# Gate and up projections by Strassen's seven block products, with rows and row sums split during attention

## The reference, cut to what matters

```python
Wg = (gate_w - 128) * gate_scale[:, None]     # 2048 x 512, integers 0..63
Wu = (up_w - 128) * up_scale[:, None]         # 2048 x 512
Wd = (down_w - 128) * down_scale[:, None]     # 512 x 2048
g = einsum('bsh,ih->bsi', layernorm(x), Wg)
u = einsum('bsh,ih->bsi', layernorm(x), Wu)
h = silu(g) * u
x = x + layernorm(einsum('bsi,hi->bsh', h, Wd))
```

## Time and profile before

| | |
|---|---|
| times of the runs | 1633.56, 1637.59, 1638.45 us; median 1637.59 |
| span of the profiled execution | 1636.3 us (its own whole time isn't among what was kept: the median stands 1.3 us above the span) |
| PE busy, share of the span | 1543.4 us, 94% |
| DVE, ACT, POOL busy | 948.3, 796.6, 596.5 us |
| first matmul of the FFN | at 951.36 us |
| end of the last matmul | at 1627.74 us |

### The profile page before, as it was taken

How to read it: one execution, slowest core, us unless ns; L and a number is a source line. 1 busy time by engine, 2 the same in 40 slices (tenths; PEclk the granted TensorE clock), 3 DMA queues, 4 the chain that set the end, 5 groups by cost and what they waited for, 6 DMA issues and landing times.

```text
span 1636.3 us, 24454 instructions
## 1 busy us (share of the span) xinstructions
PE 1543.4 (94%) x9286; PEld 642.0 (39%) x9288; DVE 948.3 (58%) x1897; ACT 796.6 (49%) x1284; POOL 596.5 (36%) x812
## 2 busy tenths in 40 slices
PE   4899999999999999999998999999999999999997
PEld 2333333333433333343332344444444444444443
DVE  5657766689666878667876333554434343434344
ACT  5356666567666666755786743232222222222222
POOL 4335664677665667746765310020000000000001
PEclk9899999999999999999999999999999999999999
DMA  4221322114421233222355431221111111111000
GB/s 180 91 53 42 83 59 53 53 62 108 122 45 28 85 98 96 73 53 50 107 168 157 129 102 40 58 97 39 45 27 52 26 52 26 52 26 52 0 26 26
DMA packets 113398, 112.26 MB, mean 69 GB/s; under 512 B 69632, under 2 KB 69632, under 8 KB 113024
## 3 DMA queue, kind: packets, MB, share of 16 engines
q1 hardware_dynamic: 113280, 110.69, 24.0%
HBM read 45.37 MB, written 25.17 MB: 43 GB/s over the span
## 4 chain that ended last, share of the span: by engine, by line
PE 72%; POOL 14%; DVE 5%; issue 5%; ACT 3%; POOLq 0%; ACTq 0%; DVEq 0%
PE ps L968 27%; PE ps L889 15%; PE ps L985 13%; PE ps L952 10%; POOL pt L1459 7%; PE ps L926 4%; DVE mcol L1247 2%; POOL rs L1379 1%; PE ps L902 1%; POOL pt L1450 1%; POOL stage L1443 1%; POOL atl L1469 1%; PE ps L910 1%; POOL rs L1376 1%; ACT tq L1074 1%
## 5 line engine op out<-in xcount | busy, mean ns | idle before, releaser
L1101 ACT ACTIVATE pt<-ps,nrm 128x512 f32<-128x512 f32 (+1 forms) x640 | 360.7, 645 | 220.6 <-PE ps L926 202.7
L968 PE MATMUL ps<-x2in,gu 128*128 128x512 f16 x2048 | 462.4, 379 | 0.0
L1247 DVE TENSOR_REDUCE mcol<-ps 128x1 f32<-128x512 f32 (+2 forms) x600 | 305.7, 575 | 149.9 <-PE ps L910 76.6
L968 PEld LDWEIGHTS ps<-x2in,gu 128*128 128x128 f16 x2048 | 200.2, 98 | 241.9 <-ACT sg L1122 0.5
L1376 POOL TENSOR_SCALAR rs<-mv 128x1 f32<-128x1 f32 x120 | 29.9, 249 | 644.7 <-DVE mv L1146 638.2
L1318 DVE SCALAR_TENSOR_TENSOR hf<-ps,usc,sg 128x512 f32<-128x512 f32 x128 | 96.1, 751 | 259.3 <-PE ps L968 245.7
L1127 ACT ACTIVATE hh<-hf 128x512 f16<-128x512 f32 x128 | 80.7, 630 | 258.1 <-DVE hf L1318 244.5
L1459 POOL TENSOR_TENSOR pt<-pt 128x1024 f32<-128x1024 f32 x84 | 203.4, 2442 | 1.8 <-ACT pt L1101 1.8
L952 PE MATMUL ps<-pt,v 128*32 128x512 f32 (+3 forms) x1536 | 189.2, 506 | 1.8 <-DVE rec L1279 1.7
L985 PE MATMUL ps<-wd,hh 128*128 128x512 f16 x496 | 188.0, 379 | 0.0
L985 PE MATMUL ps<-wd,hl 128*128 128x512 f16 x496 | 188.0, 379 | 0.0
(11 more groups left out here) (125 smaller groups left out, 1590.1 us busy)
## 6 DMA issues: line engine op xcount, KB each, us to landing
qpack<-stage SPq DMA_DIRECT2D x192, 64.0 KB, 2.0
kpack<-stage SPq DMA_DIRECT2D x192, 64.0 KB, 2.0
xr<-in_x SPq DMA_DIRECT2D x32, 256.0 KB, 2.8
x1d<-xr SPq DMA_DIRECT2D x32, 256.0 KB, 2.1
x2d<-xh SPq DMA_DIRECT2D x32, 256.0 KB, 2.0
x1in<-x1d SPq DMA_DIRECT2D x8, 1024.0 KB, 6.1
out_x<-yy SPq DMA_DIRECT2D x32, 256.0 KB, 2.0
xin<-in_x SPq DMA_DIRECT2D x24, 256.0 KB, 2.9
```

The costliest lines, as they stand in the source:

```text
L968: mm = pe.matmul(bk, GU[:, c, m, i * 128:(i + 1) * 128], x2in[:, 1 - k, p, c, :], start=p == 0 and c == 0, stop=p == 1 and c == 3)
L1101: act.activation(Pt[:, PBUF[step], h, off:512], ps[:, BANK[job], off:512], ACT.Exp, scale=esc).then_inc(s_ex, 1)
L1247: mm = dve.tensor_reduce(mcol[:, n % 2, col:col + 1], scores, AX.X, ALU.max)
```

## The change

The depth of 512 is cut in two (columns h = 0, 1 of the rows and weights), the 2048 columns of gate and of up in two (a11, a12 / a21, a22), and the rows of a batch in even and odd tiles. The four blocks of each product are then made by seven block products instead of eight (the Winograd form), from sums of row blocks and sums of weight blocks. Rows: instead of turn2 alone, pairs of tiles go norm2, turn2, mix (POOL, four subtractions of 256 columns), turnc; so `x2d` becomes four arrays, even, odd, t32, t14. XS2 = 512 takes the place of XS = 1024 as the scale of these rows. Weights: eight sums_of_weights jobs on DVE, six in the steps of the last attention unit and two behind it.

The FFN now has 64 phases (b of 4, g of 8, m: gate or up): seven products of four matmuls each into banks 0, 3, 2, 1, and again 0, 3, 2 on top. Between them ACT copies bank 0, 3 and 2 out, DVE and POOL add the shared parts. Down of the even rows runs along (8 matmuls in each phase with g > 0, banks 4 to 7); down of the odd rows follows behind the eighth group (last_down, block), in banks 0 to 3, from h2, which keeps all halves of the odd rows. Row buffers for even and t14 are double, for odd and t32 single.

```diff
+PRODUCTS = (("a11", "b11", 0), ("s3", "t3", 3), ("s1", "t1", 2), ("s2", "t2", 1), ("a12", "b21", 0), ("a22", "t4", 3),
+            ("s4", "b22", 2))
+TILES = ((0, 0), (1, 1), (1, 0), (0, 1))
+TAIL_WO = {27: 2, 28: 4, 29: 5, 30: 7, 31: 8}
 # row_work: planner
-    cost = {"ln1_stats": 9, "ln1_turn": 7, "wo_stats": 9, "residual": 17, "turn2": 7}
+    cost = {"ln1_stats": 9, "ln1_turn": 7, "wo_stats": 9, "residual": 17}
+    pairs = [[t, ["norm2", "turn2", "mix", "turnc"], 0] for t in range(0, NT, 2)]
...
+                need = {"turn2": 11, "mix": 0, "turnc": 14}[kind]
+                n, s = divmod(step, NS)
+                if kind == "mix" and (n < SUMS and 3 <= s <= 6 or pooled(n, s)) or room.get(step, 99) < need:
+                    continue
 # order_of_jobs
+            if n == NG - 1 and 4 <= s:
+                add(("sums_of_weights", s - 4))
...
+    plan += [("sums_of_weights", 6), ("sums_of_weights", 7), ("load_ds",)]
+    for b in range(B):
+        for g in range(8):
+            for m in range(2):
+                k = phase(b, g, m)
+                add(("ffn", b, g, m))
+                plan += [("woproj", t) for t, at in TAIL_WO.items() if at == k]
+                here = rows.get(NS * NG + k, [])
+                plan += [("dev", DEV_FOR[job[0]], job[1]) for job in here if job[0] in DEV_FOR]
+                plan += [job for job in here if job[0] in HALVED] + [job for job in here if job[0] not in HALVED]
+                if g > 0:
+                    add(("down", b, g - 1, m))
+                if b > 0 and shown and m == 0:
+                    add(shown.pop(0))
...
+        plan += [("block", b, 0, 0), ("last_down", b), ("block", b, 0, 1)]
+        T = 2 * b
+        plan += [("scale_out", T, 0), ("scale_out", T, 1), ("finish", T, 0), ("scale_out", T, 2), ("finish", T, 1),
+                 ("scale_out", T, 3), ("finish", T, 2), ("finish", T, 3), ("scale_out", T + 1, 0)]
+        for s in range(1, 4):
+            add(("block", b, s, 0))
+            add(("scale_out", T + 1, s))
 # tensor
+                    for k, (w, x, bk) in enumerate(PRODUCTS):
...
+                        if k >= 4:
+                            e.wait_ge(s_cp, 3 * ph + k - 3)
...
+                        elif (g, m) == (0, 0):
+                            e.wait_ge(s_y, NO["scale_out", 2 * b - 1, bk])
+                        elif bk == 0 and m == 0:
+                            e.wait_ge(s_hf, 4 * (group - 1) + 1)
+                        elif bk == 0:
+                            e.wait_ge(s_sg, 4 * group + 1)
+                        else:
+                            e.wait_ge((None, s_u2, s_c12, s_c21)[bk], ph)
...
+                        for p, c in of:
+                            mm = pe.matmul(ps[:, bk, :], weights(w, m)[:, c, g * 128:(g + 1) * 128], unit(x, b)[:, p, c, :],
+                                           start=k < 4 and (p, c) == (0, 0), stop=(p, c) == (1, 1), skip_group_check=k >= 4)
 # scalar
+                    act.activation(part1[:], ps[:, 0, :], ACT.Copy).then_inc(s_cp, 1)
...
+                    act.activation(summed[:, 1, :], ps[:, 3, :], ACT.Copy).then_inc(s_cp, 1)
...
+                    act.activation(part5[:], ps[:, 2, :], ACT.Copy).then_inc(s_cp, 1)
+                    if m == 0:
...
+                        act.activation(sg[:, 0, :], ps[:, 0, :], ACT.Silu, scale=gsc[:, g:g + 1]).then_inc(s_sg, 1)
+                        for tile in range(1, 4):
+                            e.wait_ge((None, s_c22, s_c21, s_c12)[tile], ph + 1)
...
+                    else:
+                        for tile in range(4):
...
+                            e.wait_ge(s_hf, 4 * group + tile + 1)
+                            act.activation(halves_of(b, g, tile, 0), hf[:, tile, :], ACT.Copy).then_inc(s_hh, 1)
 # vector
+                    dve.tensor_tensor(part16[:], ps[:, 1, :], part1[:], ALU.add).then_inc(s_u2, 1)
+                    if m == 1:
+                        dve.scalar_tensor_tensor(out=hf[:, 0, :], in0=ps[:, 0, :], ...
+                    dve.tensor_tensor(summed[:, 2, :], ps[:, 3, :], part16[:], ALU.add).then_inc(s_c21, 1)
+                    if m == 1:
+                        e.wait_ge(s_c22, ph + 1)
+                        dve.scalar_tensor_tensor(out=hf[:, 1, :], in0=hf[:, 1, :], ...
+                    dve.tensor_tensor(summed[:, 3, :], ps[:, 2, :], part16[:], ALU.add).then_inc(s_c12, 1)
...
+                    if m == 1:
+                        for tile in (2, 3):  # hf[2], hf[3]
...
+                        for tile in range(4):
+                            e.wait_ge(s_hh, 4 * group + tile + 1)
+                            dve.tensor_tensor(halves_of(b, g, tile, 1), hf[:, tile, :], halves_of(b, g, tile, 0),
+                                              ALU.subtract).then_inc(s_hl, 1)
 # gpsimd
+                elif kind == "mix":
+                    pool.tensor_tensor(even[:, 0:256], odd[:, 0:256], even[:, 0:256], ALU.subtract).then_inc(s_mix, 1)
+                    pool.tensor_tensor(odd[:, 0:256], odd[:, 256:512], odd[:, 0:256], ALU.subtract).then_inc(s_mix, 1)
...
+                elif kind == "ffn":
+                    e.wait_ge(s_cp, 3 * ph + 3)
+                    pool.tensor_tensor(summed[:, 1, :], summed[:, 1, :], part5[:], ALU.add).then_inc(s_q, 1)
+                    e.wait_ge(s_u2, ph + 1)
+                    pool.tensor_tensor(summed[:, 1, :], summed[:, 1, :], part16[:], ALU.add).then_inc(s_c22, 1)
```

More of the change, by code:

```diff
@@ L21 @@
 XS = 1024.0
+XS2 = 512.0
 T = 4096.0
@@ L95 @@
 LN1 = ("ln1_stats", "ln1_norm", "ln1_turn")
-LN2 = ("wo_stats", "wo_z", "residual", "norm2", "turn2")
+LN2 = ("wo_stats", "wo_z", "residual")
+HALVED = ("ln1_turn", "turn2", "turnc")
 DEV_FOR = {"ln1_norm": "ln1_stats", "wo_z": "wo_stats", "norm2": "residual"}
@@ L170, in row_work @@
             kinds.pop(0)
+        for pair in pairs:
+            t, kinds, ready = pair
+            if not kinds or ready > step:
+                continue
+            kind = kinds[0]
+            if kind == "norm2":
+                if open_pair is not None or max(at.get(("residual", t + k), step) for k in range(2)) >= step:
+                    continue
+                open_pair = t
+            else:
+                need = {"turn2": 11, "mix": 0, "turnc": 14}[kind]
+                n, s = divmod(step, NS)
+                if kind == "mix" and (n < SUMS and 3 <= s <= 6 or pooled(n, s)) or room.get(step, 99) < need:
+                    continue
+                if step in room:
+                    room[step] -= need
+                if kind == "turnc":
+                    open_pair = None
+            if kind != "mix":
+                at[kind, t] = step
+            at[kind, t + 1] = step
+            pair[2] = step + 1
+            kinds.pop(0)
+    for n in range(NG):
+        for s, job in projections(n).items():
+            assert job[0] != "woproj" or job[1] < 2 or at["residual", job[1] - 2] <= NS * n + s, job
+    for t, k in TAIL_WO.items():
+        assert at["residual", t - 2] < NS * NG + k, t
     return at
@@ L280, in order_of_jobs @@
[L280 to L293, removed]
@@ L350, with part_value @@
 for job in PLAN:
-    if job[0] == "step":
+    if job[0] in ("step", "ffn"):
         now = job
-    elif job[0] in ("ln1_turn", "turn2"):
-        ON_POOL[job] = now is not None and pooled(*now[1:])
+    elif job[0] in HALVED:
+        ON_POOL[job] = job[0] == "ln1_turn" and now is not None and now[0] == "step" and pooled(*now[1:])
+SLOT, HALF_NO, BEFORE_HALF, HALVES, latest = {}, {}, {}, [0, 0], [None, None]
+for job in PLAN:
+    if job[0] in HALVED and (job[0] != "ln1_turn" or job[1] >= 8):
+        k = sum(HALVES) % 2
+        HALVES[k] += 1
+        SLOT[job], HALF_NO[job], BEFORE_HALF[job] = k, HALVES[k], latest[k]
+        latest[k] = job
+X2_NO = {job: no + 1 for no, job in enumerate(job for job in PLAN if job[0] in ("turn2", "turnc"))}
+DOWN_NO, count = {}, 0
+for job in PLAN:
+    if job[0] == "down":
+        count += 1
+        DOWN_NO[job] = count
+    elif job[0] == "last_down":
+        for part in range(4):
+            count += 1
+            DOWN_NO[job + (part,)] = count
+    elif job[0] == "block" and job[2:] != (0, 0):
+        count += 1
+        DOWN_NO["block", job[1], job[2]] = count
+def part_value(T, s):
+    b, other = divmod(T, 2)
+    return DOWN_NO["block", b, s] if other else DOWN_NO["last_down", b, s]
 BANK, FORMER, held = {}, {}, {}
@@ L401 @@
         continue
-    elif kind in ("qk", "vproj", "woproj") and attention and not feed:
+    elif kind in ("qk", "vproj", "woproj") and attention:
         take(job, FREE[0])
@@ L570, in build @@
         x1d = nc.dram_tensor("x1d", (B * S, D), F32, kind="Internal").ap()
-        x2d = nc.dram_tensor("x2d", (B * S, 1024), F16, kind="Internal").ap()
+        x2d = {name: nc.dram_tensor("x2d_" + name, (B * S // 2, 512 if name == "odd" else 1024), F16, kind="Internal").ap()
+               for name in ("even", "odd", "t32", "t14")}
```

(6 more changed lines are left out.)

603 lines of the change are left out of this document (388 added, 215 removed).

## The result

The changed kernel takes **1655.97 us** (median of 4 runs, 1652.07 to 1663.15) against 1638.0 of the kernel before. The ratio is 1.0119, 95% interval 1.0093 to 1.0146: slower by 1.2%. 1605 us was forecast, 1587 to 1631 was the range. The profiled execution took 1652.07 us, the shortest of the four, so its trace shows some 4 us less than the median; its span is 1650.3, 14.0 more than before.

The account below looks back on a forecast made before the run. PE was taken to bound the FFN by its number of matmuls, and nearly attention. 1636.3 - 55.2 + 6 + 3 + 6 + 1 - 1 + 8 = 1604.1, + 1.3 = 1605 us; range 1587 to 1631.

Parts of the forecast that it names:

- Step 6: Attention: mixes and halves added to DVE, ACT and POOL make PE wait, +8 us, bounds 0 and 28.
- Rival B: Attention: mixes stand before masks, DVE's rows before maxima; +28 us there, 1625 in all; chance 0.28 together with C.
- Step 4: First FFN batch: ACT's rows stand between hh3 and the next phase's copies, +6 us (0 to 15).
- step 3: Start of the FFN: two weight sums on DVE delay the first phases, +3 us (1 to 6).
- Steps 1, 2, 3 and 5: FFN: 1, fewer matmuls, -55.2 us; 2, ring inside phases, +6; 3, start, +3; 5, batch borders +1, end -1.
- Matmuls: FFN: 256 matmuls fewer at 0.2158 us each, -55.2 us; a phase with down takes 7.77 us.
- Ring: FFN phases, from hh3 to the next bank copies: no wait for g > 0, 1.5 us four times at g = 0, +6.
- Batch border: Between FFN batches: bank 3 of block goes through scale_out before the second product, +1 us with batch 0's late stores.
- Start: FFN's beginning: two weight sums take 3 to 5.5 us on DVE, PE loses +3 us (1 to 6).
- A: Whole kernel: all added work hidden, terms 2 to 6 at their low bounds, 1584 us; chance 0.13.
- D: FFN: the ring from hh3 to the next copies binds in every pair of phases, 1650 us; chance 0.07.
- C: FFN: POOL's first sum meets hl3 or hf3 at the port in every pair, 1623 us; chance 0.28 together with B.

Follow-up runs that it names:

- e4: The changed kernel with the mixes and the mixed rows' halving cut to one column, all instructions and waits kept: 36 us less than the changed kernel.
- e11: e9 with the mixes and the mixed rows' halving cut to one column: 5.6 us faster than e9.
- e1: The changed kernel with three buffers xh for the float16 halves of rows instead of two: 20 us less than the changed kernel.
- e5: e1 with ACT's row jobs of the first batch's m = 1 phases issued behind the next phase's three bank copies: 1632.18 us.
- e7: e1 with the mixes kept out of step 7 too, and sixteen places of statistics instead of eight: 1621.15 us.
- e12: e9 with e10's rule for turn2 only in attention units before 12: 1609.77 us, 0.9836 of the kernel before.
- e9: The changed kernel with the edits of e7 and e5 together: 1618.74 us.
- e10: e9 with turn2 at least three steps behind its normalisation and in no step of an ln1_turn: median 2 us over the range 1614 to 1622.
- e3: The changed kernel with at most one halving of an input tile (ln1_turn) per step in steps 3 to 7: 18 us slower than the changed kernel.

## Why the prediction was wrong

The direction, the size and the range failed, and one step did most of it. The median missed the 1605 us by 51. Against the forecast span of 1604.1 the profiled one is 46.2 us longer, and its parts can be taken one by one.

**Step 6, attention, failed: +8 forecast, 28 the upper bound, +46.9 measured; 39 of the 46 us.** The text said that the FFN's start after 970 would show this step wrong, and it was 998.3. The amount of work was about right: ACT +8.8 us, DVE +26, POOL +32 where 11, 21 and 24 were forecast. DVE's has six weight sums of 1.2 us in it, and POOL's subtraction of 256 columns took 0.72 us where I had 0.6. What failed is the rate: I turned 56 us of work into waits "at the average, times four". But there is no such rate: the amount cost 26.6 us in one order (e4) and 1 to 2 in another (e11). What a piece costs is set by what it holds and what stands behind it. Three kinds of such waits weren't in the sum, or were priced too low:
- *a buffer*: 3 halves in a step, 2 buffers `xh`. The text counted halves and stores and never asked how long a buffer is held. The earlier trace rows already had ACT waiting for `xT<-xh`. e1: 16.4 us of attention (9.1 by e5's execution);
- *the place of a mix* behind the block sums, late for ACT and ahead of masks. Rival B had the mechanism and priced it at POOL's own duration; e7 against e1: 11 us (18 against e5);
- *halvings too close to each other*: `turn2` too soon behind its normalisation or in a step of another tile's halving, which fills even three buffers. e12 against e9: 10 us, of which 8.4 in units 5 to 11, where e10 has the same; the other 2 are of the size of scatter.

Each was measured on top of the one before. The three come to 37 of 48, 11 stay open in place. Unit 14 has 7.4 of these, with the same wait in e12 (7.2 us) as in the change, where two stores of `x2d_t` issued at 929.94 free their buffer only at 936.4, with weight loads on both sides of them in SP's list. That it is these loads wasn't tried.
The bound of 28 was none: it took each mix once before a mask. It left out that a late buffer or load passes its delay to the next maxima or exponentials and so to PE, and that the clock then falls (85.3 us at 1.2 GHz, 41.0 before), so that the price of a gap nearly doubles. e3 and e10 show the first in one chain each, the windows around 411 us the second.

**Step 4, rows in batch 0: +6 forecast, up to 15; about +17.6 measured.** The batch lost 20.4, of which 2.8 are gaps in its first 18 us (step 3). The place was right, ACT's rows ahead of the next copies: e5 moved them and won 6.2. The size was not: half of ACT's 21 us were priced by their own durations, without ACT's waits inside them (2.05 for L1679 above), and 10.2 us of the batch ran at 1.2 GHz. e9 still loses 13.4 over its matmuls, and e11 (less work there) 9.7; what makes up that rest stays open.

**Steps 1, 2, 3 and 5 held.** Matmuls: 7.77 us per phase, to the hundredth. Ring: no wait in the pairs with g > 0. At g = 0, forecast 1.5 us, PE waited 0.47:
```profile
1199.31 0.69 DVE L1614 TENSOR_TENSOR h2a<-hf,h2a 128x512 f16<-128x512 f32 x1
1199.37 0.58 ACT L1342 ACTIVATE part<-ps 128x512 f32<-128x512 f32 x1
...
1200.00 1.04 PE L1163 MATMUL ps<-x2even,gu 128*128 128x512 f16 x4 [0.47 <-ACT part L1342]
```
A copy takes 0.58 us where I had 0.63 to 0.68. Batch border and ring together: 0.9 per batch, 1.8 forecast. Start: the two weight sums of 2048 float16 that stand behind attention take 2.76 us, the lower of my two bounds (1.4 each):
```profile
1001.17 2.76 DVE L1573 TENSOR_TENSOR sw<-gu,sw 128x2048 f16<-128x2048 f16 x2
```
PE lost about 2.8 us there with g = 0's wait in it, 4.5 forecast.

**The rivals.** A (1584) and D (the ring binds, 1650) fell in the FFN: D's time was nearly met, but by another mechanism, so that was luck. C, the port in every pair, fell too:
```profile
L1614 DVE TENSOR_TENSOR h<-hf,h x64: 679/685/690, 1017.0 to 1613.2; 128x512 f16<-128x512 f32 x64
L1586 DVE TENSOR_TENSOR part<-ps,part x64: 671/692/693, 1003.9 to 1607.0; 128x512 f32<-128x512 f32 x64
L1712 POOL TENSOR_TENSOR sg<-sg,part x32: 1260/1268/1350, 1004.9 to 1599.0; 128x512 f32<-128x512 f32 x32
```
The lower halves (L1614), which C had meeting POOL's first sum, never took over 0.690; POOL's sums kept to 1.35 and the DVE operations with a PSUM input beside them to 0.693. B was nearest in its mechanism, but its price was an average too, and I gave the sum of all such cases, an attention that loses more than the FFN gains, no chance of its own: the slower side had 0.06, held by D alone. The 8 us had come out of a multiplication with no row behind it, and a term like that should have had the FFN's whole gain of 40 us inside its range.

## What to carry to other kernels

Row work spread beside a bound engine isn't priced by its busy time or by room on one engine. For each piece, ask what holds its buffer, what stands behind it in each in-order list, the DMA queue's too, and who waits for that. Here the same work cost attention 48 us in one order with two buffers and 11 in another with three. When a change moves work into a stretch that was full, the first thing to try is one more buffer and another step, before the arithmetic is judged; and postponing a job isn't free, since the loads that are issued with it are postponed too.

## What the runs showed of the hardware

- A POOL operation on one column, 0.26 us typically, took 4.80 us while DVE ran operations with two on-chip inputs one after another. DVE in that time (start, us, engine, line, operation):
```profile
1115.06 1.41 DVE L1610 SCALAR_TENSOR_TENSOR hf<-hf,usc,sg 128x512 f32<-128x512 f32 x2
1116.38 0.69 DVE L1614 TENSOR_TENSOR h<-hf,h 128x512 f16<-128x512 f32 x1
...
1118.79 1.29 DVE L753 TENSOR_TENSOR xh<-xn,xh 128x512 f16<-128x512 f32 x2
```
POOL came free at 1120.13, where the last of them ended (1120.08). The Trainium skill, page "SBUF — State Buffer", section "Who interferes with whom", says that a VectorE instruction with two SBUF inputs contends with a GpSimd instruction that reads SBUF. These rows agree, and add that the one that waits can wait out a chain of eight instructions, not one.
- A gap of 3.33 us in PE (at 411 us) left a mean granted clock of 0.82 over the next 15.3 us; it was 1.00 before.
- Two executions with the same order of attention differed there by 7.3 us (e1, e5).
